# A fused embedding, attention and mixture-of-experts kernel on one core: the order of its engines at the head, in attention's steps and at attention's end

## The reference

```python
h = concat([cls, patches @ W.T + b]) + pos                # 197 rows of an image
h = concat([h, emb2[hash2] + emb3[hash3] + emb4[hash4]])   # + 32 rows of text
h = h + gau(layernorm(h))     # xn = x/|x|*g; u, v, base = split(silu(xn @ uv_w));
                              # q, k = base*gamma + beta; kern = relu((q k^T + rel)/sqrt(128))^2
                              # x*res_scale + (u * (kern @ v)) @ o_w
h = h + moe(layernorm(h))     # 2 shared experts on every row; of 8 routed ones the top 2
                              # by softmax(x @ gate), weighted; each 128 -> 512 -> gelu -> 128
```

## Time and profile before

| | |
|---|---|
| median of 3 runs | 1250.35 us (1245.68 to 1252.9) |
| the profiled execution | 1243.88 us |
| its span | 1242.2 us |
| PE busy | 1169.7 us, 94% |
| DVE busy | 970.1 us, 78% |
| POOL busy | 840.9 us, 68% |
| ACT busy | 807.6 us, 65% |
| DMA | 143.53 MB, mean 116 GB/s |

### The profile page before, as it was taken

The page is one execution under the profiler, slowest core; times in us unless marked ns, Lnnn a source line. Parts: engine busy times, 40 slices in busy tenths (PEclk is TensorE's granted clock), DMA queues, the critical chain, the costliest instruction groups (busy, mean ns, idle before and its releaser), DMA issues.

```text
span 1242.2 us, 32105 instructions
## 1 busy us (share of the span) xinstructions
PE 1169.7 (94%) x9514; PEld 886.8 (71%) x9514; DVE 970.1 (78%) x2516; ACT 807.6 (65%) x1867; POOL 840.9 (68%) x808
## 2 busy tenths in 40 slices
PE   4999999999999999868999988999999999999998
PEld 2777777777777777644555447999999889964555
DVE  5688898888888888757987765777777767778997
ACT  2566666666665566535555545777777777768877
POOL 4435776666677776546887784777777777776564
PEclk8999999999999999979999998999999999999999
DMA  6233444444444442223444424544555444439998
GB/s 179 81 113 115 129 132 132 131 132 126 119 134 128 131 121 74 67 73 101 112 114 128 111 62 88 98 97 99 93 95 92 92 97 96 90 81 189 204 201 165
DMA packets 208056, 143.53 MB, mean 116 GB/s; under 512 B 119036, under 2 KB 186745, under 8 KB 207892
## 3 DMA queue, kind: packets, MB, share of 16 engines
q1 hardware_dynamic: 166868, 93.93, 30.1%
q0 software_dynamic: 36992, 40.97, 15.4%
q10 hardware_dynamic: 4032, 6.57, 2.1%
HBM read 70.38 MB, written 55.96 MB: 102 GB/s over the span
## 4 chain that ended last, share of the span: by engine, by line
PE 33%; POOL 32%; issue 24%; SPq 4%; DMA 3%; ACT 3%; DVE 1%; POOLq 0%; ACTq 0%; DVEq 0%
POOL slots_dram L483 9%; POOL slots_dram L1544 4%; POOL y_dram L1555 4%; POOL rstd L524 3%; PE bank L1832 3%; PE bank L1856 3%; PE bank L1857 3%; PE bank L1855 3%; PE bank L1834 3%; PE bank L1833 3%; PE bank L1263 2%; POOL rstd L530 2%; PE bank L1264 2%; PE bank L1265 2%; PE bank L1304 2%
## 5 line engine op out<-in xcount | busy, mean ns | idle before, releaser
L1555 POOL DMA_INDIRECT y_dram<-y_sb,y_row x244 | 268.3, 1100 | 92.7 <-issue 74.1
L1640 ACT ACTIVATE gel_all<-bank,b 128x256 f32<-128x256 f32 x488 | 191.8, 475 | 49.7 <-PE bank L1834 47.7
L1271 ACT ACTIVATE gel_all<-bank,b 128x458 f32<-128x458 f32 x256 | 154.8, 640 | 83.5 <-PE bank L1265 56.2
L1855 PE MATMUL bank<-w_part_hi,hid_all 128*128 x976 | 170.5, 219 | 0.0
L1857 PE MATMUL bank<-w_part_hi,hid_all 128*128 x976 | 169.9, 219 | 0.0
L1856 PE MATMUL bank<-w_part_lo,hid_all 128*128 x976 | 169.9, 219 | 0.0
L1762 DVE CAST hid_all<-gel_all 128x1024 f16<-128x1024 f32 x122 | 85.6, 702 | 107.0 <-ACT gel_all L1640 107.0
L483 POOL DMA_INDIRECT slots_dram<-row_bufs,slot_1st x128 | 129.9, 1015 | 39.2 <-issue 39.2
L1764 DVE TENSOR_TENSOR hid_all<-gel_all,hid_all 128x1024 f16<-128x1024 f32 x122 | 149.5, 1225 | 4.2
L1544 POOL DMA_INDIRECT slots_dram<-row_bufs,slot_2nd x104 | 125.6, 1208 | 31.6 <-issue 31.0
L1282 DVE TENSOR_TENSOR hid_all<-gel_all,hid_all 128x916 f16<-128x916 f32 x128 | 142.4, 1113 | 4.4
(11 more groups left out here) (190 smaller groups left out, 3001.8 us busy)
## 6 DMA issues: line engine op xcount, KB each, us to landing
xin<-in_xmain SPq DMA_DIRECT2D x32, 771.8 KB
x2r_dram<-row_bufs SPq DMA_DIRECT2D x32, 260.0 KB, 2.1
x2t_dram<-x2T SPq DMA_DIRECT2D x32, 229.0 KB, 2.9
row_bufs<-x2r_dram SPq DMA_DIRECT2D x26, 260.0 KB, 2.9
x_cols<-x2t_dram ACTq DMA_DIRECT2D x28, 229.0 KB, 2.8
stage<-in_ffn_w SPq DMA_DIRECT2D x20, 256.0 KB
xin<-in_xrest SPq DMA_DIRECT2D x32, 128.6 KB
y_dram<-y_sb,y_row POOLq DMA_INDIRECT x244
```

The costliest lines, as they stand in the source:

```text
L1271: act.activation(self.gel[:, f // 2 % 2, f % 2, :], self.up_dst(k, f), ACT.Gelu, bias=self.b1[:, f:f + 1]).then_inc(self.gel_ready, 1)
L1555: pool.indirect_dma_start(out=y_dram, in_=y_sb[:, s, c, :], in_offset=None, out_offset=bass.IndirectOffsetOnAxis(ap=y_row[:, s, c:c + 1], ...
L1640: act.activation(gel[:, s8 % 2, f, :], up_bank[s8 % 2][half][:, (f % 2) * TILE:(f % 2 + 1) * TILE], ACT.Gelu, bias=of_expert(b1, SHARED * ...
L1855: pe.matmul(part, h_hi, w2_hi, start=False, stop=False)
```

## The change

Six edits of order; no instruction is added or removed apart from where it stands.
1. POOL: `scatter_rows` always issues its four DMAs in one batch. In step 31 the power of the last pair (`mid_powers(31)`) stood between the second and the third of them; it stands behind all four now.
2. POOL: from step 32 on `keep_top(i - 2)` stands behind `scatter_rows(i - 4)`, not ahead of it.
3. DVE: in a step, `top(i - 1)` stands ahead of `halves_low(i - 1)`.
4. ACT: the wait for the row buffer and the copy of the token numbers go from `second_norm` to `halves_hi`; `halves_hi(i - 1)` goes from its place ahead of `scaled_rows(i + 2)` to behind `copy_h(i + 3)`.
5. ACT's tail: `between(act, 0)` (four Gelus of the shared experts) goes ahead of `second_norm(31)`, and `columns_hi(31)` ahead of `halves_hi(31)`.
6. PE's head: `patches(2)` goes from step -1 to step -2, ahead of `xn_columns(0)` and `to_rows(1)`.

```diff
@@ -473,11 +473,11 @@
                 pool.tensor_tensor(block_on_chip(i, 1), stage[:, 0:WBLOCK], block_on_chip(i, 0),
                                    ALU.subtract).then_inc(ws_done, 1)
 
-            def scatter_rows(b, g, buf, chunks=range(4)):
+            def scatter_rows(b, g, buf):
                 pool.wait_ge(slots_up, g + 1)
                 pool.wait_ge(rows_ready, b + 1)
                 settle(pool)
-                for c in chunks:
+                for c in range(4):
                     m = CHUNKS[c % 2][1]
                     at = buf % 2 * 4 + c
                     pool.indirect_dma_start(
@@ -532,14 +532,12 @@
             def step(i, p, j, q):
                 last_ahead = p == 0 and (not isinstance(j, int) or 0 <= j + 2 < IMGS // 4)
                 text_ahead = p == 1 and (not isinstance(j, int) or 0 <= j + 3 < IMGS // 4)
-                if exists(i - 2):
+                if i < PAIRS and exists(i - 2):
                     keep_top(i - 2)
-                if i == PAIRS - 1:
-                    scatter_rows(i - 4, j - 2, q, range(2))
-                    mid_powers(i)
-                    scatter_rows(i - 4, j - 2, q, range(2, 4))
-                elif exists(i - 4):
+                if exists(i - 4):
                     scatter_rows(i - 4, j - 2, q)
+                if i >= PAIRS and exists(i - 2):
+                    keep_top(i - 2)
                 if text_ahead:
                     gather_text(j + 3)
                 if last_ahead:
@@ -549,7 +547,7 @@
                 k, half = again(i - 1)
                 if k is not None:
                     scatter_again(k, half)
-                if exists(i) and i < PAIRS - 1:
+                if exists(i):
                     mid_powers(i)
                 if exists(i + 3):
                     front_powers(i + 3, 1 - p)
@@ -801,9 +799,9 @@
                 if exists(i + 2):
                     xnT_low(i + 2, p)
                 if exists(i - 1):
+                    top(i - 1, 1 - p)
+                if exists(i - 1):
                     halves_low(i - 1, (q - 1) % 4)
-                if exists(i - 1):
-                    top(i - 1, 1 - p)
                 if p == 0 and exists(i - 2):
                     choose(j - 1)
                 if i == AGAIN_AT - 2:
@@ -917,11 +915,6 @@
 
             def second_norm(b, buf):
 
-                if reaches(b, ROW_BUFS):
-                    act.wait_ge(r_out[buf], 4 * (b - buf))
-                    act.wait_ge(scattered[buf], 16 * (b - buf))
-                act.activation(rows_1st[:, buf, :, HID:HID + 1], token_1st[:, bass.ds(4 * b, 4)].rearrange("p (c o) -> p c o", o=1),
-                               ACT.Copy)
                 act.wait_ge(shift2_ready, b + 1)
                 if reaches(b, 1):
                     act.wait_ge(tr3_done, b)
@@ -933,6 +926,11 @@
 
             def halves_hi(b, buf):
 
+                if reaches(b, ROW_BUFS):
+                    act.wait_ge(r_out[buf], 4 * (b - buf))
+                    act.wait_ge(scattered[buf], 16 * (b - buf))
+                act.activation(rows_1st[:, buf, :, HID:HID + 1], token_1st[:, bass.ds(4 * b, 4)].rearrange("p (c o) -> p c o", o=1),
+                               ACT.Copy)
                 act.wait_ge(x2_ready, b + 1)
                 act.activation(rows_16[:, buf, :, 0:HID], x2_rows[:, :, :], ACT.Copy).then_inc(rows_hi, 1)
 
@@ -963,8 +961,6 @@
                     uv(i + 1, 1 - p, 2)
                 if exists(i - 1) and drains(i):
                     columns_hi(i - 1, 1 - p)
-                if exists(i - 1):
-                    halves_hi(i - 1, (q - 1) % 4)
                 if exists(i + 2):
                     scaled_rows(i + 2, p)
                 if exists(i + 3) and p == 1:
@@ -973,6 +969,8 @@
                     copy_xnT(i + 2, p)
                 if exists(i + 3):
                     copy_h(i + 3, 1 - p)
+                if exists(i - 1):
+                    halves_hi(i - 1, (q - 1) % 4)
                 if exists(i + 1):
                     uv(i + 1, 1 - p, 3)
                     uv(i + 1, 1 - p, 4)
@@ -994,10 +992,10 @@
             second_norm(b - 1, (b - 1) % ROW_BUFS)
             columns_hi(b - 1, 0)
             halves_hi(b - 1, (b - 1) % ROW_BUFS)
+            between(act, 0)
             second_norm(b, b % ROW_BUFS)
+            columns_hi(b, 1)
             halves_hi(b, b % ROW_BUFS)
-            between(act, 0)
-            columns_hi(b, 1)
             between(act, 1)
 
         def tensor(pe, between):
@@ -1148,10 +1146,13 @@
                     uv(i + 1, 1 - p, 0)
                 if exists(i):
                     av(i, 0)
-                if exists(i + 3) and i != -2:
+                if i == -3:
+                    patches(0, 0, j)
+                    patches(1, 1, j)
+                elif i == -2:
+                    patches(2, 0, j)
+                elif i >= 0 and exists(i + 3):
                     patches(i + 3, 1 - p, j)
-                if i == -3:
-                    patches(1, 1, j)
                 if exists(i):
                     av(i, 1)
                 if exists(i - 1) and not drains(i):
```

## The result

| | before | after |
|---|---|---|
| median of 20 runs | 1250.19 us (1245.39 to 1255.23) | 1244.63 us (1237.22 to 1250.99) |
| ratio | | 0.9953, 95% interval 0.9939 to 0.9968: 5.9 us less (4.0 to 7.6) |
| the profiled execution | 1243.88 us | 1247.93 us, span 1246.1 |

The change gains 5.9 us by the ratio (the two medians are 5.6 apart), just short of the 0.5% named in the prediction. Stage by stage they can, up to the start of the shared experts. Most lines of the changed kernel stand two lower in attention (L1033 is L1031) and one higher in the experts.

What follows compares the result with a forecast made beforehand. Attention's middle was taken to be bound by TensorE with two late suppliers. Head +3.5, steps -2.8 and drain -8.5 sum to -7.8 us, a median of 1242.5 us; the 8-in-10 range was 1234 to 1251.

Steps and rivals of the forecast that it cites:

- Head: Start of the kernel: patches(2) moved earlier costs +3.5 us, +1.6 for the later text and +1.9 for the clock.
- Rival 1: Head: TensorE keeps its clock or its gap matters less, so the head costs 0; time 1239 us, chance 0.2.
- Steps: Attention's odd and even steps: each pair gains 0.20 us, not 0.52, because of the text sum; -2.8 us in all.
- Drain: End of attention: the reordered scatters, stores, Gelus and keep_top together gain 8.5 us, bounds -10 and -5.5.
- (a): Drain: scatter_rows(27) as one batch ahead of the last power; cost 0, at most 0.6 us.
- (b): Drain: halves_low(29) behind top, so the x_cols load is issued 1.45 us later; +1.4 for all that follows.
- (c): Drain: ScalarE's early table load and Gelus end TensorE's wait of 8.28 us; with (b), x2_columns(31) comes 7.3 us earlier.
- (d): Drain: without the long gap TensorE needn't run at 1.2 GHz from 565.0 to 568.5; 1.2 us gained.
- (e): Drain: keep_top behind scatters 28 and 29; scatter 28 ends at about 557.1, scatter 30 starts 8 us earlier.
- Rival 2: Routed tiles: the drain's gain isn't passed on through GpSimd's second scatters; +0.7 in all, 1251 us, chance 0.2.
- Rival 3: Steps: halves_low makes VectorE the bound, 0.60 in each of 29 steps, 17.4 us; time 1263 us, chance 0.08.

Runs made afterwards that it cites:

- e10: Kernel before with only the head's change, patches(2) one step earlier: 1439.35 us, ratio 1.0016.
- e1: Changed kernel with only the head's change undone, patches(2) back in step -1: 1448.72 us, ratio 1.0061 to the kernel before.
- e5: The kernel of e1 run again, on another chip: 1424.53 us, ratio 1.0145 to the kernel before.
- e2: Kernel before with only ScalarE's move in the steps (buffer waits, token copy and halves_hi behind copy_h): 1438.21 us, ratio 1.0008.
- e4: Kernel before with only ScalarE's tail reordered (Gelus ahead of the second norm, columns_hi ahead of halves_hi): 1430.59 us, ratio 0.9956.
- e11: Kernel before with only the changes at attention's end (GpSimd's scatters and keep_top, ScalarE's tail): 1430.01 us, ratio 0.9950.
- e8: Changed kernel with the head's change and VectorE's swap undone: 1430.93 us, ratio 0.9978 to the kernel before.
- e12: The kernel of e8 run again: 1434.47 us, ratio 0.9995 to the kernel before.
- e9: Kernel before with only VectorE's swap, top ahead of halves_low: 1458.79 us, ratio 1.0156.

## Why the prediction was right, and where it wasn't

**Head, predicted +3.5: right, 3.9, or 3.7 from `to_rows(0)` on.** Both pauses are in the trace, both at the places and with the lengths named. Counted from `to_rows(0)` the text came 1.6 later (1.6 was said) and the clock cost 2.0 (1.9). The edit alone gives the same: e10 has 21.75 against 18.28 to 18.49, that is 3.3 to 3.5, and a median 2.4 higher, which its interval doesn't quite set apart from nothing. Rival 1 (the head keeps its clock) falls: all three traces with the edit show 21.4 to 21.9. The rule of the Trainium skill quoted for it ("TensorE: Matmul & The Clock Gate", What's actually happening), that the moment of a change varies, does show, but against the unedited head: in e1 the granted clock stays at 0.50 until 32.0, and the head takes 19.22 (19.24 in e5, the same kernel). Two stretches of e1:

```profile
22.00:29.00 7.00, 3.08 (x12) 2.20 (x13) 3.52 (x15) 3.88 (x7) 2.70 (x2) 0.50 0.12 35
29.00:32.00 3.00, 3.00 (x6) 1.59 (x5) 1.93 (x8) 2.18 (x4) 2.28 (x2) 0.50 0.01 3
```

**Steps, predicted -2.8: right on the first chip, -3.3.** The wait at the transposes to rows shrank by 0.5 each time, and the text sum took its place, as said: 4.5 us against 0.9, so a pair gives 0.25 and not 0.52. That is read from two traces; no run isolates it on such a chip. On the others e2 has the same smaller wait and gives nothing, since TensorE waits there for v instead (36.7 us; 19.7 to 31.5 in e4 and e10) and VectorE for the rounded rows.

**Drain, predicted -8.5: too much, -6.2.** Edit (a) cost nothing: the power waits 1.22 for its statistics. The `x_cols` load (b) came 1.3 later against the last text transpose (1.45 was said). The Gelus (c) do end the wait of 8.28. The early table load (547.71) was not what ended last.

The term that was mis-sized is the clock. (c) reckoned the logits of pair 30 and `up(0,3)` at full clock, and (d) counted -1.2 more. But the clock fell in the pause ahead of these logits. The twelve logits matmuls took 1.32 from the first start to the last end (0.80 before), so `up(0,3)` came at 550.26, not at 549.2 and the 0.6 by which attention was late. Then `up(0,3)` and the eight matmuls behind it start 0.38 apart, as they did from 556 and from 565 before. ScalarE's last Gelu waits 0.89 for the first three of them, which take 0.6 longer than at full clock, and the norm of 31 stands behind it. These two, 0.5 and 0.6, are what is missing from the -7.3 of (c). The -1.2 of (d) didn't come either: the slow stretch from 565 stands at 559.1 to 562.5 now, with seven matmuls in it instead of nine.

The pause itself was not new, as the row from 544.72 above shows. New is another of 2.01 in front of it, ahead of the first matmuls on `x_cols` (0.43 before), which comes from (b). But e5, with the same order of work from the steps on, has pauses of 2.11 and 2.18 at these two places, and the clock stays up through both and through `up(0,3)` (until 616.2):

```profile
607.80:610.00 2.20, 0.04 (x1) 0.04 (x1) 2.06 (x11) 2.17 (x5) 0.89 (x2) 1.00 0.09 28
610.00:614.00 4.00, 2.82 (x24) 1.68 (x25) 3.56 (x22) 3.65 (x8) 0.50 (x1) 1.00 0.33 125
```

So the 1.1 us are what one execution lost; whether the clock falls there in most of them is open. On the other chips, with `halves_low(29)` in its old place, the end's edits gave 8.4. That is close to 8.5 by luck: (b) is missing there, and without its 1.45 the predicted terms would make 9.9. In e11 the clock fell in the same pause as well (granted 0.57 from 600.5 to 604.5).

Of (e), scatter 28 ended at 559.43 and not at 557.1, and VectorE's `top(31)` waited 1.28 us for the `keep_top` behind it; GpSimd's last first scatter still comes 4.7 earlier.

**Sum.** 3.9 - 3.3 - 6.2 is -5.6 at `x2_columns(31)`, and the medians say the same at the end of the program (-5.9 by the ratio). These are two different measurements: no trace shows where the medians' gain stands, and the traced execution lost its own behind this point. Against the predicted -7.8 the clock at the end is the largest error; head and steps were off by 0.4 and 0.5 with opposite signs.

**Rival 2 (the end's gain isn't passed on): true in one execution, not in the medians.** Of the profiled execution's 5.56 us, 4.66 are left at the first of GpSimd's last 104 second scatters (580.59 against 585.25) and 1.80 at the last: each takes 1.24 us on average instead of 1.21, the longest 1.97 instead of 1.58. The medians over 20 runs differ by as much as the whole gain. e4 and e11 speak against the rival too: their ends are 6.6 and 8.4 us shorter, and their medians 6.8 and 7.0 lower. How often the chain gives the gain back isn't settled.

**Rival 3 (`halves_low` makes VectorE the bound): its mechanism is shown, on the other chips.** The place, the price (0.60 a step, 17.4 us; measured 0.65 a step, 17.0 in 26 of them) and the point from which it decides (a norm later than the 0.7 us of slack) were those of the prediction. That the price fits so well is partly luck: `picked` beside GpSimd's split, which the prediction had not priced, can make up as much as 3.6 of the 17.0 us (12 times 0.651 less 0.354), and part of the 0.60 is hidden in some steps. Its argument against, that VectorE waits for the logits anyway, holds only while the logits come in time; where they are 1.5 us late (in e10's odd step VectorE takes them 2.36 us after TensorE's first logits row, 212.03 to 214.39; on the first chip 0.81 after it, 196.14 to 196.95), the old order spent that wait on `halves_low` and the new one adds it behind. On the first chip, in the step shown, the rival was 0.1 us away. I gave it 0.08 because I asked only whether the slack was used up, not how little disturbance it would take.

**A version without the loss.** e11, the end alone, takes 0.5% off the kernel before on these chips, where the changed kernel adds 1.1%. On the first chip it wasn't run; since head and steps nearly cancel there (+3.9 and -3.3), it should be about as fast as the changed kernel, and that is argued, not shown. e8 and e12, with ScalarE's move besides, can't be told from no change.

## What to carry to other kernels

Work that stands ahead of a wait is free only there; behind the wait it is in series, and its whole length counts as soon as the slack behind it is gone, so price a swap by the slack that it leaves and not by the time that it takes. Filling one pause of TensorE from the work that had filled the next only moves the pause, and each of them can cost a stretch at half clock. Where several small reorderings come in one change, take each alone: here the end's edits made the gain, the head's gave back more than half of it, and VectorE's lost over twice as much on another chip.

## What the runs showed of the hardware

- **The same program differed by 15% between the chips it met, and a change's sign with it.** The kernel before took 1250.19, 1403.59 and 1437 us, the changed one 1244.63 (ratio 0.9953) and 1453.52 (1.0110). Durations of single instructions hardly differ; what differs is TensorE being late at the logits, which VectorE's rows show as waits of 2.56 us released by nothing that the profile names ("remote"). Its cause is open, and so is whether it belongs to the chip, since each chip stands in one group of runs only.
- **VectorE's `picked` took 0.91 us when GpSimd's split had started before it, and 0.28 when it started first** (e9: split 218.29, `picked` 218.78; e10: `picked` 216.05, split 216.16), on average 651 ns in e9 against 354 in e10. In e9 it ended at 219.69, 0.14 after the split. The Trainium skill ("SBUF — State Buffer", SBUF: two separate sides) says that VectorE and GpSimd share a pair of ports as an exclusive lock, taken by whichever instruction starts first, for VectorE's instructions with two inputs in SBUF too, against a GpSimd instruction that reads SBUF; both are so here, and the rows agree. So the order of one engine also decides what it collides with.
- **The same pause of 2.18 us cost the clock in one trace and not in another.** In the changed kernel TensorE had nothing to do from 546.9 to 549.08; the granted clock was 1.00 from 546 to 548, 0.92 from 548 to 549 and 0.50 from 549 to 550.2, and stayed there until 555.5. In the kernel before (544.72 to 546.90) and in e5 (607.78 to 609.96) it was 1.00 all through the pause and in the logits behind it. So a gain that rests on a short pause keeping its clock should be entered with both outcomes.
